# Four attention layers on one core: ACT rounds the norms' columns, and DVE's remainder of the third norm stands later in its step

## The reference, cut to what matters

```python
tgt2 = _linear(_attention(q, k, v, tgt_mask), o_w, o_b)        # self attention, 16 heads of 16
x = _layernorm(tgt + tgt2, ln1_g, ln1_b)                       # norm 1
q = _linear(x, cq_w, cq_b)
k = _linear(memory, ck_w, ck_b)
v = _linear(memory, cv_w, cv_b)
tgt2 = _linear(_attention(q, k, v, None), co_w, co_b)          # cross attention
x = _layernorm(x + tgt2, ln2_g, ln2_b)                         # norm 2
tgt2 = _linear(jax.nn.relu(_linear(x, lin1_w, lin1_b)), lin2_w, lin2_b)
x = _layernorm(x + tgt2, ln3_g, ln3_b)                         # norm 3
```

## Time and profile before

| what | value |
|---|---|
| median of 3 runs | 3716.16 us |
| the profiled execution's own time | 3719.9 us |
| its span in the trace | 3718.2 us |
| granted clock, mean | 0.94 |
| PE busy | 3191.6 us (86%) |
| DVE busy | 2138.0 us (58%) |
| ACT busy | 1879.8 us (51%) |
| POOL busy | 1654.9 us (45%) |

### The profile page before, as it was taken

How to read it: one execution, slowest core, us unless ns; L and a number is a source line. 1 busy time by engine, 2 the same in 40 slices (tenths; PEclk the granted TensorE clock), 3 DMA queues, 4 the chain that set the end, 5 groups by cost and what they waited for, 6 DMA issues and landing times. The chain is left out here.

```text
span 3718.2 us, 79408 instructions
## 1 busy us (share of the span) xinstructions
PE 3191.6 (86%) x27248; PEld 2726.8 (73%) x27248; DVE 2138.0 (58%) x4222; ACT 1879.8 (51%) x7766; POOL 1654.9 (45%) x2020
## 2 busy tenths in 40 slices
PE   8999996899999997379999999737999999966887
PEld 5998995688888887267877777626888888754664
DVE  2555553444444444357777777525777777744665
ACT  2444442334333333256666666425676666634775
POOL 1223221024444445235666666622566666662544
PEclk8999998999999998689999999968999999988999
DMA  3111112110111110211112111021111111103331
GB/s 105 51 51 65 59 37 105 57 37 24 48 48 48 48 46 32 105 47 55 52 57 61 56 57 54 21 102 41 49 49 53 53 55 55 41 29 100 93 97 54
DMA packets 192554, 213.62 MB, mean 57 GB/s; under 512 B 30208, under 2 KB 161536, under 8 KB 189696
## 3 DMA queue, kind: packets, MB, share of 16 engines
q1 hardware_dynamic: 192384, 211.40, 17.9%
HBM read 131.59 MB, written 58.72 MB: 51 GB/s over the span
## 5 line engine op out<-in xcount | busy, mean ns | idle before, releaser
L1641 ACT ACTIVATE second_stage<-second_psum,second_neg_max 128x128 f32<-128x128 f32 x1024 | 362.9, 392 | 245.7 <-DVE second_neg_max L1621 245.5
L1641 ACT ACTIVATE third_stage<-third_psum,third_neg_max 128x128 f32<-128x128 f32 x1024 | 362.5, 388 | 224.4 <-DVE third_neg_max L1621 224.3
L1641 ACT ACTIVATION_READ_ACCUMULATOR second_stage<-second_psum,second_neg_max 128x1 f32 x1024 | 237.5, 232 | 0.0
L1641 ACT ACTIVATION_READ_ACCUMULATOR third_stage<-third_psum,third_neg_max 128x1 f32 x1024 | 233.8, 228 | 0.0
L534 POOL TENSOR_TENSOR cross_ff_hidden_lo<-cross_ff_relu,cross_ff_hidden_hi 128x256 fp32r<-128x256 f32 x128 | 93.2, 729 | 289.4 <-DVE cross_ff_hidden_hi L529 289.4
L1621 DVE TENSOR_REDUCE second_neg_max<-second_psum 128x4 f32<-128x512 f32 x256 | 169.2, 684 | 61.9 <-PE second_psum L1584 60.2
L1621 DVE TENSOR_REDUCE third_neg_max<-third_psum 128x4 f32<-128x512 f32 x256 | 168.8, 682 | 41.8 <-PE third_psum L1584 40.7
L1524 ACT ACTIVATE fourth_stage<-fourth_psum,fourth_neg_max 128x128 f32<-128x128 f32 x512 | 181.8, 386 | 3.5 <-DVE fourth_neg_max L1500 3.5
L1595 PE MATMUL third_psum<-third_eye,third_stage 128*128 128x128 f32 x1024 | 163.2, 283 | 15.7 <-DVE third_p_turned_odd L1627 7.9
L1595 PE MATMUL second_psum<-second_eye,second_stage 128*128 128x128 f32 x1024 | 162.4, 282 | 14.7 <-DVE second_p_turned_odd L1627 7.5
L529 DVE CAST cross_ff_hidden_hi<-cross_ff_relu 128x256 fp32r<-128x256 f32 x128 | 44.9, 351 | 212.4 <-ACT cross_ff_relu L524 212.4
(11 more groups left out here) (438 smaller groups left out, 12637.7 us busy)
## 6 DMA issues: line engine op xcount, KB each, us to landing
second_stage<-second_a_k SPq DMA_DIRECT2D x512, 16.0 KB, 1.8
third_stage<-third_a_k SPq DMA_DIRECT2D x512, 16.0 KB, 1.8
cross_arena<-in_l0b_packed SPq DMA_DIRECT2D x6, 1024.0 KB, 4.9
self_arena<-in_l0a_packed SPq DMA_DIRECT2D x4, 1024.0 KB, 6.3
self_x_raw<-in_x_t SPq DMA_DIRECT2D x8, 512.0 KB, 3.7
self_x_rows<-in_x_rows SPq DMA_DIRECT2D x8, 512.0 KB, 3.8
self_ct_raw<-in_ctx_t SPq DMA_DIRECT2D x8, 512.0 KB, 4.3
context_hi<-self_ct_hi SPq DMA_DIRECT2D x8, 512.0 KB, 4.9
```

Source lines behind the costliest of these rows:

```text
L1641: ins = act.activation(self.sh.p_wide[:, 4 * b + t, x, :], psum[:, SCORE_BANKS[t], x * SEQ:(x + 1) * SEQ], ACT.Exp, bias=self.sh.neg_max[: ...
```

## The change

`dve_split` is taken apart. The rounding copy becomes `act_hi` on ACT, directly behind `act`. The subtraction becomes `dve_lo` on DVE; it waits for ACT's copy. For norms 1 and 2 `dve_lo` keeps the place of `dve_split`. For norm 3 it moves behind `proj2.dve_v` and `turned(x0[1], 3)`, and ACT's copy now waits, too, for the store of the round before to have ended (`stored`).

```diff
-    def dve_split(self, dve, r, stored=None):
+    def act_hi(self, act, r, stored=None):
+        if stored is not None:
+            act.wait_ge(stored.sem, stored.at(r, 0))
+        act.wait_ge(self.turned_ready.sem, self.turned_ready.at(r, 1))
+        act.copy(self.yt.hi[:], self.y[:]).then_inc(self.hi_ready.sem, 1)
+
+    def dve_lo(self, dve, r, stored=None):
         if stored is not None:
             dve.wait_ge(stored.sem, stored.at(r, 0))
-        dve.wait_ge(self.turned_ready.sem, self.turned_ready.at(r, 1))
-        dve.tensor_copy(self.yt.hi[:], self.y[:]).then_inc(self.hi_ready.sem, 1)
         dve.wait_ge(self.hi_ready.sem, self.hi_ready.at(r, 1))
         dve.tensor_tensor(self.yt.lo[:], self.y[:], f32(self.yt.hi[:]),
                           ALU.subtract).then_inc(self.lo_ready.sem, 1)
@@ ACT
                 if ok(-4):
                     norm3.act(act, Back(r, 4), psum)
+                    norm3.act_hi(act, Back(r, 4), stored)
                 exp(x0_next, 0)
...
                 if ok(-2):
                     norm2.act(act, Back(r, 2), psum)
+                    norm2.act_hi(act, Back(r, 2))
                 exp(x1_next, 2)
                 exp(x1_next, 3)
...
                 if ok(0):
                     norm1.act(act, r, psum)
+                    norm1.act_hi(act, r)
                 exp(y1_next, 2)
@@ DVE
                 turned(x0[1], 2)
-                if ok(-4):
-                    norm3.dve_split(dve, Back(r, 4), stored)
                 if ok(-1):
                     proj2.dve_v(dve, Back(r, 1), psum)
                 turned(x0[1], 3)
+                if ok(-4):
+                    norm3.dve_lo(dve, Back(r, 4), stored)
...
                 if ok(-2):
-                    norm2.dve_split(dve, Back(r, 2))
+                    norm2.dve_lo(dve, Back(r, 2))
...
                 if ok(0):
-                    norm1.dve_split(dve, r)
+                    norm1.dve_lo(dve, r)
```

## The result

The changed kernel takes **3671.78 us**, the median of 4 runs (3667.35 to 3681.04), against 3717.93 us for the kernel before in as many. The ratio is 0.9887, 95% interval [0.9864, 0.9909]: 1.1% faster. The profiled execution took 3672.43 us, its span is 3670.7 us. The forecast was 3674 us, in a range from 3656 to 3692.

What follows compares the result with a forecast made beforehand. The prediction took PE to set the time in the steady rounds, DVE work as such being worth nothing. Its terms, -36.0 + 8.0 - 17.1 = -45 us, took 3719.9 to 3675; it forecast 3674 us, range 3656 to 3692.

Steps and rivals of the forecast that it cites:

- The wait goes, -36.0 us: End of x0: PE's wait on `a_v` falls from 1.91 to 0.41 us in 12 + 12 rounds, -36.0 us.
- The subtraction at its new place, 0: Behind `turned 3` in x0: norm 3's subtraction, about 0.7 us, fits DVE's 1.28 us idle gap; cost 0.
- The falls of the clock, -17.1 us: Steady rounds of both programs: drops of PE's clock behind the 1.91 us wait go with it, -17.1 us.
- The rival in which they stay: Clock falls stay at their present rate behind the 0.41 us wait or norm 2's; 3688 us, chance 0.14.
- ACT's copies, +8.0 us: Hidden in x0 and x1; in y1 norm 1's copy loses 0.19 us a round, 0.66 in first two; +8.0 us.
- The delay in the first rounds: First two rounds of each program, y1: no feed-forward instruction covers norm 1's copy on ACT, so each loses 0.66 us.
- ACT's copy, 0.59 us: Each 128 x 512 rounding copy on ACT takes 0.59 us, read from a copy out of PSUM taking 585 ns.
- Norm 2's subtraction, 0: In x1: it still ends behind POOL's residual sum, so its end and PE's wait stay; 0.
- The rival in which the subtraction slips in ahead: In x1: norm 2's subtraction starts before POOL's residual sum, PE's waits go, 16 us more, 3658 us; chance 0.10.
- The sum: All terms together: -36.0 + 8.0 - 17.1 = -45 us for the whole kernel.
- Slower by ACT: ACT releases PE in every step: 0.66 us at three places in 32 rounds, +27 us, 3743; chance 0.04.
- the wait that doesn't go: Something else keeps DVE from `a_v`, only the copies' cost is left: 3724 us; chance 0.04.

Runs made afterwards that it cites:

- the wait put back: Three DVE memsets of 128 x 768 put ahead of `dve_v` in the changed kernel, otherwise unchanged; 3695.6 us, 0.9946 of the kernel before.
- the residual first: Changed kernel, but on POOL the residual sum of x1 stands ahead of the attention's subtraction; 3663.4 us, 0.9855 of the kernel before.
- nothing moved: All three copies on ACT, but norm 3's subtraction left ahead of the read of the values; 3674.3 us, 0.9892 of the kernel before.

## Why the prediction was right, point by point

- *The wait goes, -36.0 us.* Right: 1.91 to 0.41 us in every round. I call the time from one norm's transposes to the next one's a leg. In a round at full clock the leg that holds the wait, from norm 3's to norm 2's, went from 20.63 to 19.13 us. But the reason given, that the split leaves the place ahead of `a_v`, is only one of two that suffice. With the subtraction left there and only the copy gone, the wait is 0.52 us. The row that says so stood there, POOL's 1.33 us instruction in the earlier trace rows; I did not ask what an earlier start of the subtraction would do to its turn.
- *The subtraction at its new place, 0.* Right: 0.68 us, 0.66 left of the gap.
- *The falls of the clock, -17.1 us.* Right in size: no steady round has one. The rival in which they stay is out, and the wait put back shows that the length of the wait decides.
- *ACT's copies, +8.0 us.* This term was mis-sized. In the steady rounds the leg from norm 1's transposes to norm 3's, with the end of y1 in it, grew by 0.17 us (0.19 forecast). There the size was right, but the path was not: PEld's wait for ACT ahead of the fourth mask product, which was to grow from 0.51 to 0.7 us, stayed at 0.47 to 0.51. The delay reaches PE at an earlier instruction: norm 3's transposes write EV_BANK, which the feed-forward instruction reads. They start 0.13 us behind its end in the steady rounds of both kernels, and that end moved; PE in before, then ACT, PE and PEld in after:

```profile
1951.51 0.65 PE L1729 MATMUL second_psum<-second_eye,second_n_z 128*128 128x128 f32 x4
...
1941.47 0.85 ACT L1803 ACTIVATE second_ff_relu<-second_psum,second_cols 128x256 f32<-128x256 f32 x2
...
1942.45 0.65 PE L1729 MATMUL second_psum<-second_eye,second_n_z 128*128 128x128 f32 x4
...
1943.77 0.10 PEld L1576 LDWEIGHTS second_psum<-second_mask_flags,second_mask_eye 128*128 128x128 bf16 x1 [0.47 <-ACT second_stage L1641]
```

  The delay in the first rounds was right as well, 0.68 us against 0.66, where the clock didn't fall. What the step left out is the clock: the delay makes a third wait beside two of 1.0 us, and the clock fell behind it. The fills cost 3.8 + 5.8 = 9.6 us where the forecast had 2 x (2 x 0.66 + 0.19) = 3.0 for them.
- *ACT's copy, 0.59 us.* It is 0.62; ACT's row for the second program:

```profile
L1746 ACT CAST second_n_yt_hi<-second_n_y x48: 617/621/626, 1606.9 to 2411.8; 128x512 fp32r<-128x512 f32 x48
```

  The table in "VectorE: DVE Perf Modes" (the Trainium skill, "The TRN2 errata - SBUF-src ops pay a fixed extra latency per instruction") charges 224 cycles and one per element at 1.2 GHz, which makes an estimate of 613 ns for this copy out of SBUF. The trace has 621, within 8 ns of it, and my row, a copy out of PSUM with 585 ns, was the worse guide.
- *Norm 2's subtraction, 0.* Nearly: it does end behind POOL's residual, as forecast, but PE's wait fell from 0.78 to 0.51 us (6.1 / 12), and the leg from norm 2's transposes to norm 1's by 0.23 us in the second program and 0.16 in the third. DVE and POOL of after at that place, then DVE's copy in before, next to the earlier trace rows:

```profile
1868.23 1.63 DVE L1752 TENSOR_TENSOR second_n_yt_lo<-second_n_y,second_n_yt_hi 128x512 fp32r<-128x512 f32 x1 [0.39 <-ACT second_n_yt_hi L1746]
...
1868.03 1.28 POOL L2006 TENSOR_TENSOR second_residual<-second_x_rows,second_rows 128x512 f32<-128x512 f32 x1
...
2076.33 0.59 DVE L1746 CAST second_n_yt_hi<-second_n_y 128x512 fp32r<-128x512 f32 x1
```

  POOL's residual takes 1.28 us, not the 1.47 of the earlier trace rows: in before DVE's copy started 0.27 us ahead of POOL's 2076.60, and by the same pattern as above it had held POOL up; no run tests this by itself. The rival in which the subtraction slips in ahead missed by 0.20 us (1868.03 against 1868.23), close to the 0.17 worked out. What it promised, 16 us, is of the size of the 11.8 us that the residual first gave.
- *The sum.* For the 22 steady rounds: -33 for the wait (22 x 1.50), -17.1 for the falls, +3.7 for ACT (22 x 0.17) and -4.3 for norm 2's wait (11 x 0.23 + 11 x 0.16) make -50.7; measured -50.4. With +9.6 in the fills and -6.1 in the tails (3.0 of it the twelfth round's wait) the whole is -47 us against -45. That the total came nearer than its terms is luck: the loss in the first rounds, 6.6 us over its forecast, and the gains that were put at nothing nearly cancelled.
- *Slower by ACT, and the wait that doesn't go:* out, by the waits of after.

## What to carry to other kernels

When a DVE instruction with two SBUF inputs is far longer than its kind, look which POOL instruction it ended behind; a place where POOL is quiet, or a turn one POOL instruction earlier, can be worth more than moving work to another engine. Before moving work to an idle engine ask what the move itself buys: here the same split, only reordered on its old engine, gave more than the whole gain (1.4% against 1.1%) without loading ACT. And look at the written-out first rounds apart from the steady ones, since there an idle engine's cover is missing, and short PE waits stand close together.

## What the runs showed of the hardware

- **Waits and PE's clock.** In the steady rounds a single wait of 1.91 us was followed by a stretch at 1.2 GHz in 13 of 22 rounds, one of 1.92 to 1.94 us in 14 of 22, one of 1.41 us in none of 22. In the fill, waits of 1.04, 0.61 and 1.01 us with 1.1 and 0.4 us of work between them were followed by a fall in nine stretches of twelve; the same stretch with two waits of 1.04 and 1.00 us had one in one of fourteen. A fall cost 0.7 to 1.7 us in a round and 2.7 to 4.0 us in the fill (25.34 and 26.63 less 22.65), more than the third wait of 0.61 us there.
- **POOL is held by DVE too.** Its residual sum of 128 x 512 took 1.28 us in after and 1.47 in before, where DVE's copy had started 0.27 us ahead of it. Its second rows instruction took 1.27 us in after and 1.60 with nothing moved, where DVE's subtraction ended 0.47 us after its start.
- **DVE's copy alone** of 128 x 512 takes 0.42 us where POOL is quiet, and 1.49 in the earlier trace rows, beside POOL's first rows instruction.
